# A residual load asked for eight halves later in one slot of an attention and expert block

## The chip, the cores and the metric

One core of one Trainium2 chip. The metric is the device time of one execution in microseconds, as the median of the runs shown. Lower is better.

## The reference, cut to what matters

The input x has 4 batches of 1024 tokens with 512 features. A block of attention (16 heads of 32) with a residual and a layer norm is followed by a routed low-rank expert block with a residual and a layer norm.

```python
xq, xk, xv = x @ wq.T, x @ wk.T, x @ wv.T             # split into 16 heads of 32
scores = einsum('bqhd,bkhd->bhqk', xq, xk)            # not scaled
probs = softmax(scores, axis=-1)
x = layernorm(x + einsum('bhqk,bkhd->bqhd', probs, xv).reshape(4, 1024, 512) @ wo.T)
# experts: E = 8, rank 64, out 512
logits = x @ Wr.T + br
h = einsum('nd,erd->ner', x, A)
y = einsum('ner,eor->neo', h, B) / 64
out = layernorm(x + y[argmax(logits)] * max(softmax(logits)))
```

## The kernel before

The attention of a pair of heads over one batch is a slot: 4 batches by 8 pairs are 32 slots, numbered 0 to 31. A slot has 16 units (8 blocks of keys by two heads), and a unit has two halves of 512 queries, so a slot has 32 halves, called h = 0 to 31 in the code. Each half makes one score product (`sc`, line 767), one exponential on ScalarE (`P`, line 894) and one product for the row maxima of the next slot (`mx`, line 757), which VectorE reduces (line 1034). Slot 8 is the first pair of the second batch, and slot 9 the second pair.

TensorE fills the room between the scores with chunks of other work by a plan that is written out at build time: projections of q, k and v (`w`, line 636), and in the slots of a later batch the output projection and the experts of the batch before. Slot 8 holds the projections of v of batch 1; slot 9 starts with the output projection of batch 0 (`o`, line 671), whose tiles VectorE adds to the residual in `r_f` (line 1134).

The denominators of the softmax go a longer way. GpSimd adds the 16 blocks of exponentials of a slot two by two into sums (lines 544 and 547), waiting for each unit's exponentials. In the next slot TensorE sums them over the keys (`den`, line 730), in slot 9 in the half h = 3; it waits there for the last add of slot 8. TensorE works through its program in order, so the attention product of slot 8 (`pv`, line 779) and the output projection stand behind it. VectorE copies the denominators (`den_s`, line 1075), SyncE spreads them over partitions (line 453), VectorE takes the reciprocals (line 1086), SyncE stores them to memory (`den_parts`, line 458) and, when the store has landed, loads them back to `den_s` (line 463). GpSimd multiplies the attention output with them in `normalise` (line 579), which waits for that load. For slot 7 this is at the half h = 19 of slot 8: `spread_den` is at h = 7, `store_rec` at h = 14, `load_rden` at h = 15. The adds of slot 8 that come later stand behind `normalise` on GpSimd.

SyncE also loads, in its one queue, the operands of the slots to come (`stack`, line 421): in slot 8 at h = 14, three transfers of 256 KB just ahead of `store_rec`. At h = 27 it issues four transfers of 4 KB with the maxima's rows (line 444); the first score of the next slot waits for them (`m_loaded`).

ScalarE issues the large loads in its own queue: the residual of the batch before, 2 MB (`load_res`, line 857), at h = 12 of slots 8, 16 and 24, and one more in slot 25; in slot 9 the experts' weights (line 865) at h = 1 and x for the next batch (line 845) at h = 3 and 9. `load_res(0)` waits for `qk_ready` 16 and for the stored slices of the weights, since `r` held the raw weights before. `load_res(1)` and `load_res(2)` wait for stored outputs. The only users of `r_loaded` are VectorE's additions in `add_attention` and `add_part`.

Of the kernel before, what the change touches and what calls it, by code (L numbers as in the profile page):

```python
# [6 lines left out]
def build_attention_lora_moe_block(nc, xT, x, wqT, wkT, wvT, woT, aT, bT, wrT, br, out):  # L7
# [130 lines left out]
    for s in range(SLOTS):  # L138
        chunks = [(kind, n, c) for kind, n in PLAN[s] for c in range(CHUNKS[kind])]
        begin, end, spent, total = FROM.get(s, 0), TO.get(s, HALVES), 0, sum(cost(kind) for kind, _, _ in chunks)  # L140
        for kind, n, c in chunks:
            half = HALVES * s + begin + int((end - begin) * (spent + cost(kind) / 2) / total)
            AT.setdefault(half, []).append((kind, n, c))
            if c + 1 == CHUNKS[kind]:
                ENDS.setdefault(half, []).append((kind, n))
            spent += cost(kind)
        ORDER += [piece for piece in PLAN[s] if piece[0] not in SHORT]
# [4 lines left out]
    for half in range(HALVES * SLOTS):  # L152
        s, h = divmod(half, HALVES)
# [46 lines left out]
    for half in range(HALVES * SLOTS):  # L200
        s, h = divmod(half, HALVES)
# [38 lines left out]
    def ends(half, kind):  # L240
        return [n for k, n in ENDS.get(half, ()) if k == kind]

    ctx = ExitStack()
    with ctx:
# [587 lines left out]
        def _(act):  # L832
# [6 lines left out]
            def load_x(b, c):  # L839
                if b and c == 0:  # L840
                    act.wait_ge(qk_ready, 16 * b)
                    act.wait_ge(v_ready, KB * b)
                elif c:
                    act.wait_ge(x_loaded[0], 16 * (b + 1))
                act.dma_start(xT_f[:, 1, :, 512 * c:512 * c + 512],
                             xT_w[:, :, S * b + 512 * c:S * b + 512 * c + 512]).then_inc(x_loaded[c], 16)

            def load_res(b):
                if b + 1 == B:
                    act.wait_ge(qk_ready, 16 * B)  # L850
                    act.wait_ge(v_ready, KB * B)
                elif b:
                    act.wait_ge(out_stored, 64 * b)
                else:
                    act.wait_ge(qk_ready, 16)
                    act.wait_ge(slices_stored, 32 * SLICES)
                act.dma_start(res(b), tokens(x, b, 0, KB)).then_inc(r_loaded, 16)

            def load_ab(b):

                act.wait_ge(v_ready, KB * (b + 1))
                if b == 1:
                    act.wait_ge(wv_stored, 16)
                for s, d in ((a_s, aT), (b_s, bT)):
                    act.dma_start(s, d.rearrange("(k p) n -> p k n", p=128)).then_inc(ab_loaded, 16)

            def load_wv(b):
                act.wait_ge(z_ready, KB * (b - 1))
                act.dma_start(wide[:, :, :, :].bitcast(f32), wv_d).then_inc(wv_loaded, 16)

            def x_high(b, m):
                c, kt = divmod(m, KT)
                act.wait_ge(x_loaded[c], 16 * (b + 1))
                act.activation(xT_s[:, 0, kt, 512 * c:512 * c + 512], xT_f[:, 1, kt, 512 * c:512 * c + 512],
                               ACT.Copy).then_inc(x_hi, 1)
# [9 lines left out]
            def exp(unit, c):  # L885
                if c == 0 and unit >= NP:
                    old, k = divmod(unit - NP, UNITS)
                    act.wait_ge(pv_done, (unit - NP) // 2 + 1)
                    if k < adds(old) + 2:
                        act.wait_ge(*summed(unit - NP))  # L890
                    else:
                        act.wait_ge(den_done, old + 1)
                act.wait_ge(sc_ready, 2 * unit + c + 1)
                act.activation(P[:, unit % NP, 512 * c:512 * c + 512], sc[c][:, :], ACT.Exp).then_inc(exp_done, 1)  # L894

            def hi_part(n):
                act.wait_ge(qk_ready, n + 1)
                before = n - (2 if n < 16 else 1)
                if before == 15:
                    act.wait_ge(qk_stored[0], 16 * 8)  # L900
                if before >= 0:
                    act.wait_ge(qk_stored[before % 2], 16 * (before // 2 + 1))
                act.activation(parts(n)[:, 0, :], BANK["qk", n][:, :], ACT.Copy).then_inc(hi_done, 1)

            def copy_v(n):
                act.wait_ge(v_ready, n + 1)
                if n >= KB:
                    act.wait_ge(pv_done, KB * (PAIRS * (n // KB) - 1) + n % KB + 1)
                act.activation(V[:, n % KB, :], BANK["v", n][:, :], ACT.Copy).then_inc(v_done, 1)

            def copy_out(s):
                act.wait_ge(pv_done, KB * (s + 1))
                if s > 1:
                    act.wait_ge(norm_done, 2 * (s - 1))
                act.activation(pv_s[:, s % 2, :], pv[:, :], ACT.Copy).then_inc(pv_copied, 1)  # L915

            def copy_max(q):
                act.wait_ge(mt_ready, q + 1)
                if q:
                    act.wait_ge(m_loaded, 64 * q)  # L920
                act.activation(mrow[:, 0, :], BANK["max_t", q][0:2 * KB, 0:128], ACT.Copy).then_inc(mhi_done, 1)

            def copy_yT(n, bank):
                act.wait_ge(t1_ready, n + 1)
                if n:
                    act.wait_ge(h_ready, n)
                act.activation(yT[:, :], bank[:, :], ACT.Copy).then_inc(yT_done, 1)

            def copy_hmT(n, bank):
                act.wait_ge(t2_ready, n + 1)  # L930
                if n:
                    act.wait_ge(z_ready, n)
                act.activation(hmT[:, :], bank[:, :], ACT.Copy, scale=SCALING).then_inc(hmT_done, 1)

            def softmax_sum(n):
                act.wait_ge(eq_done, n + 1)
                if n > 1:
                    act.wait_ge(lrec_done, n - 1)
                act.activation(lexp[:, :], logits[:, :], ACT.Exp, bias=nlmax[:, :], accum_out=lsum[:, n % 2:n % 2 + 1]).then_inc(lexp_done, 1)

            def layer_norm(kind, n):
                b, t = divmod(n, KB)
                act.wait_ge(nmr_done, NORM[kind, n] + 1)
                act.activation(res(b)[:, t, :], res(b)[:, t, :], ACT.Identity, bias=nmr[:, t:t + 1],
                               scale=rstd[:, t:t + 1]).then_inc(out_done if kind == "z" else y_done, 1)
# [27 lines left out]
            for half in range(HALVES * SLOTS):  # L973
                unit, c = divmod(half, 2)
                s, k = divmod(unit, UNITS)
                exp(unit, c)
                b, p, h = s // PAIRS, s % PAIRS, half % HALVES
                if half in LOAD_X:
                    load_x(*LOAD_X[half])
                if h == 12 and p == 0 and b:  # L980
                    load_res(b - 1)
                if h == 2 and p == 1 and b + 1 == B:
                    load_res(b)
                if h == 1 and p == 1 and b:
                    load_ab(b)
                if h == 2 and p == 7 and 0 < b < B - 1:
                    load_wv(b + 1)
                if half % HALVES == MAX_AT and s < LAST:
                    copy_max(s + 1)
                for n in ends(half - 4, "lg"):  # L990
                    softmax_sum(n)
                if c == 1 and k == 1 and s:
                    copy_out(s - 1)
                for kind, n in ENDS.get(half, ()):
                    if kind == "qk":
                        hi_part(n)
                    elif kind == "v":
                        copy_v(n)
                    elif kind == "t1":
                        copy_yT(n, BANK[kind, n])  # L1000
                    elif kind == "t2":
                        copy_hmT(n, BANK[kind, n])
                if half in X_HIGH:
                    x_high(*X_HIGH[half])
                for kind, late in (("o", 7), ("z", 11)):
                    for m in range(2):
                        for n in ends(half - late + m, kind):
                            if n % 2:
                                layer_norm(kind, n - m)
# [282 lines left out]
```

## Time and profile before

| | us |
|---|---|
| median of 3 runs | 1524.68 |
| lowest, highest | 1523.99, 1529.59 |
| the profiled execution | 1531.46 |
| its span | 1529.6 |

In the span TensorE is busy 1476.3 us (97%), GpSimd 1158.6 (76%), VectorE 935.0 (61%) and ScalarE 777.2 (51%); the mean granted clock of TensorE is 0.988 of full. The share of a busy engine is an average over the span, and single stops show only in the timeline. In the rows below the engines are PE (TensorE, PEld for its weight loads), DVE (VectorE), ACT (ScalarE), POOL (GpSimd) and SP (SyncE); SPq and ACTq are the issues of transfers on the queues of SyncE and ScalarE. L857 is line 857 of the kernel.

### The profile page before, as it was taken

How to read it: one execution, taken by the hardware profiler on the slowest of the kernel's cores; microseconds unless marked ns; L12 is line 12 of the kernel's file. 1: busy time of each engine (PE TensorE's matmuls, PEld its weight loads, DVE VectorE, ACT ScalarE, POOL GpSimd, SP SyncE). 2: the span in 40 equal slices, each digit the busy share in tenths (PEclk: the TensorE clock that was granted, in tenths of full speed). 3: DMA queues.
4: the chain of work that ended last, by engine and by line, in shares of the span. 5: the costliest groups of instructions: out<-in, count | busy, mean ns of one | idle time of the engine just before them, and what ended most of it. 6: DMA issues, size and time to landing. Idle time of an engine off the chain costs nothing.

```text
span 1529.6 us, 20559 instructions
## 1 busy us (share of the span) xinstructions
PE 1476.3 (97%) x6872; PEld 863.2 (56%) x6872; DVE 935.0 (61%) x1754; ACT 777.2 (51%) x1421; POOL 1158.6 (76%) x654
## 2 busy tenths in 40 slices
PE   7999999999899999999999999999999999999898
PEld 5755556656455655556655555555665555544354
DVE  6747666765466666666566565666556666564643
ACT  3455656655355554555556454554555555555332
POOL 0367879999698777877889887778888998889401
PEclk9999999999999999999999999999999999999999
DMA  7345634553522332326262233224335222111001
GB/s 225 106 129 152 218 80 142 152 155 89 172 60 59 91 102 65 112 77 215 57 181 67 83 85 105 84 69 137 121 103 159 49 49 57 52 40 36 8 14 42
DMA packets 80216, 153.13 MB, mean 100 GB/s; under 512 B 19040, under 2 KB 26224, under 8 KB 79728
## 3 DMA queue, kind: packets, MB, share of 16 engines
q1 hardware_dynamic: 67936, 125.07, 28.7%
q10 hardware_dynamic: 11840, 25.69, 5.1%
q8 instruction: 55, 0.90, 0.2%
q0 software_dynamic: 336, 1.07, 0.2%
q14 instruction: 49, 0.40, 0.1%
HBM read 102.52 MB, written 48.49 MB: 99 GB/s over the span
## 4 chain that ended last, share of the span: by engine, by line
PE 78%; issue 9%; POOL 7%; DVE 4%; ACT 1%; DMA 1%; SPq 0%; ACTq 0%; POOLq 0%; DVEq 0%
PE w L636 14%; PE pv L779 13%; PE sc L767 13%; PE mx L757 12%; PE w L671 6%; PE w L715 5%; PE w L702 5%; POOL Psum L547 4%; PE mx L730 2%; DVE mxc L1034 2%; POOL attT_f L579 1%; POOL Psum L544 1%; PE mx L715 1%; PE w L679 1%; PE mx L695 1%
## 5 line engine op out<-in xcount | busy, mean ns | idle before, releaser
L1034 DVE TENSOR_REDUCE mxc<-mx 128x1 f32<-128x512 f32 x1024 | 683.4, 686 | 472.6 <-PE mx L757 470.0
L894 ACT ACTIVATE P<-sc 128x512 f32<-128x512 f32 x1024 | 598.6, 596 | 516.7 <-PE sc L767 490.2
L547 POOL TENSOR_TENSOR Psum<-Psum,P 128x1024 f32<-128x1024 f32 x296 | 695.8, 2377 | 30.8 <-ACT P L894 28.5
L767 PE MATMUL sc<-stack 98*128 98x512 f32 x1024 | 539.2, 529 | 4.4 <-ACT P L894 4.0
L757 PE MATMUL mx<-stack 96*128 96x512 f32 x1024 | 405.0, 401 | 5.4 <-DVE mxc L1034 2.8
L767 PEld LDWEIGHTS sc<-stack 98*128 98x128 f32 x1024 | 194.2, 190 | 139.6 <-issue 83.2
L757 PEld LDWEIGHTS mx<-stack 96*128 96x128 f32 x1024 | 195.6, 191 | 115.6 <-issue 69.5
L779 PE MATMUL pv<-P,V 128*32 128x512 f32 x2048 | 252.7, 612 | 0.0
L636 PE MATMUL w<-xT_s,wqk_s 128*128 128x512 f32 x624 | 199.1, 410 | 12.0 <-DVE xT_s L1051 10.4
L544 POOL TENSOR_TENSOR Psum<-P 128x1024 f32<-128x1024 f32 x50 | 118.5, 2384 | 117.4 <-ACT P L894 108.9
L636 PEld LDWEIGHTS w<-xT_s,wqk_s 128*128 128x128 f32 x624 | 117.7, 193 | 70.0 <-issue 45.5
L779 PEld LDWEIGHTS pv<-P,V 128*32 128x32 f32 x2048 | 57.6, 111 | 131.5 <-issue 106.6
L636 PE MATMUL w<-wide,xT_s 128*128 128x512 f32 x384 | 114.0, 400 | 0.0
L702 PE MATMUL w<-wide_f,turned_f 128*128 128x512 f32 x208 | 108.0, 605 | 0.0
L547 POOL TENSOR_TENSOR xT_s_f<-xT_s_f,P 128x1024 f32<-128x1024 f32 x41 | 97.1, 2391 | 13.3 <-ACT P L894 12.9
L715 PE MATMUL w<-wide_f,turned_f 128*128 128x512 f32 x208 | 106.9, 599 | 0.1
L671 PE MATMUL w<-wo_s,attT_f 128*128 128x512 f32 x198 | 102.4, 599 | 0.0
L579 POOL TENSOR_TENSOR attT_f<-pv_s,den_s 64x512 f32<-64x512 f32 x62 | 80.1, 1291 | 25.5 <-issue 17.7
L636 PEld LDWEIGHTS w<-wide,xT_s 128*128 128x128 f32 x384 | 71.2, 190 | 28.4 <-issue 13.4
L547 POOL TENSOR_TENSOR wo_s<-wo_s,P 128x1024 f32<-128x1024 f32 x32 | 75.3, 2384 | 2.4 <-ACT P L894 2.1
L556 POOL TENSOR_TENSOR ve<-mv,eps_s 128x2 f32<-128x2 f32 (+1 forms) x33 | 6.5, 196 | 87.6 <-DVE mv L1123 87.6
L915 ACT ACTIVATE pv_s<-pv 128x512 f32<-128x512 f32 x32 | 19.1, 597 | 75.1 <-PE pv L779 75.1
(146 smaller groups left out, 1090.2 us busy)
## 6 DMA issues: line engine op xcount, KB each, us to landing
stack<-qk_parts SPq DMA_DIRECT2D x186, 256.0 KB, 4.3
qk_parts<-split SPq DMA_DIRECT2D x56, 512.0 KB, 3.3
wqk_s<-wqk_parts SPq DMA_DIRECT2D x24, 512.0 KB, 4.4
den_s<-den_parts SPq DMA_DIRECT2D x124, 64.0 KB, 2.0
xT_s_f<-xT ACTq DMA_DIRECT2D x6, 1024.0 KB, 6.8
r_f<-x ACTq DMA_DIRECT2D x3, 2048.0 KB, 12.8
out<-r_f SPq DMA_DIRECT2D x12, 512.0 KB, 3.4
qk_parts<-turned SPq DMA_DIRECT2D x8, 512.0 KB, 2.8
```

Source lines behind the costliest of these rows:

```text
L544: pool.tensor_tensor(sums(s)[:, i, :], P[:, (unit - 2) % NP, :], P[:, unit % NP, :], ALU.add).then_inc(add_done, 1)
L547: pool.tensor_tensor(sums(s)[:, i, :], sums(s)[:, i, :], P[:, unit % NP, :], ALU.add).then_inc(add_done, 1)
L579: pool.tensor_tensor(attT[64 * (p % 2):64 * (p % 2) + 64, p // 2, 512 * c:512 * c + 512], pv_s[64 * c:64 * c + 64, s % 2, :], den_s[64 * c ...
L636: return pe.matmul(bank[:, :], weights[i], moving[j], start=(c == 0), stop=(c == PASSES * KT - 1))
L671: done = pe.matmul(bank[:, :], attT[:, kt, 128 * t:128 * t + 128], wo_s[:, kt, :], start=(kt == 0 or only), stop=(kt == KT - 1))
L702: done = pe.matmul(bank[:, :], yT[:, 128 * kt:128 * kt + 128], a_s[:, kt, :], start=(kt == 0), stop=(kt == KT - 1))
L715: done = pe.matmul(bank[:, :], hmT[:, 128 * kt:128 * kt + 128], b_s[:, kt, :], start=(kt == 0), stop=(kt == KT - 1))
L757: pe.matmul(bank[:, :], stack(q, i)[0:3 * HD, 1, 128 * qb:128 * qb + 128], stack(q, i)[0:3 * HD, 0, 512 * c:512 * c + 512], start=True, st ...
L767: pe.matmul(sc[c][:, :], stack(s, i)[0:KS, 0, 128 * kb:128 * kb + 128], stack(s, i)[0:KS, 1, 512 * c:512 * c + 512], start=True, stop=True ...
L779: done = pe.matmul(pv[at:at + HD, :], V[:, kb, HD * head:HD * head + HD], P[:, (UNITS * s + 2 * kb + i) % NP, 512 * c:512 * c + 512], star ...
L894: act.activation(P[:, unit % NP, 512 * c:512 * c + 512], sc[c][:, :], ACT.Exp).then_inc(exp_done, 1)
L1034: dve.tensor_reduce(mxc[:, q % 2, at:at + 1], BANK["max", g][:, :], AX.X, ALU.max).then_inc(mx_done, 1)
```

## The change

`load_res(0)` is called in slot 8 at h = 20 instead of h = 12. The calls in slots 16 and 24 stay at h = 12, and the one in slot 25 stays where it is.

```diff
                 if half in LOAD_X:
                     load_x(*LOAD_X[half])
-                if h == 12 and p == 0 and b:
+                if h == (20 if b == 1 else 12) and p == 0 and b:
                     load_res(b - 1)
                 if h == 2 and p == 1 and b + 1 == B:
                     load_res(b)
```

## Rows read from the trace of the kernel before

**Rows 1.** The page, part 1: busy us (share of span) xinstructions of each engine.

```profile
PE 1476.3 (97%) x6872; PEld 863.2 (56%) x6872; DVE 935.0 (61%) x1754; ACT 777.2 (51%) x1421; POOL 1158.6 (76%) x654
```

**Rows 2.** Waits, 372 to 440 us: total us, times, longest us.

```profile
PE mx L730 <- POOL Psum L547: 6.8, 1, 6.8
```

**Rows 3.** Timeline of GpSimd: start us, us, instruction, count, [idle before <-releaser].

```profile
380.87 7.11 POOL L547 TENSOR_TENSOR Psum<-Psum,P 128x1024 f32<-128x1024 f32 x3 [0.57 <-ACT P L894]
395.88 2.64 POOL L579 TENSOR_TENSOR attT_f<-pv_s,den_s 64x512 f32<-64x512 f32 x2 [7.91 <-issue]
398.59 16.31 POOL L547 TENSOR_TENSOR Psum<-Psum,P 128x1024 f32<-128x1024 f32 x7
```

**Rows 4.** Timeline of TensorE's products at the start of slot 9.

```profile
407.81 0.39 PE L757 MATMUL mx<-stack 96*128 96x512 f32 x1
415.04 1.94 PE L730 MATMUL mx<-Psum,ones 128*32 128x512 f32 x8 [6.84 <-POOL Psum L547]
...
419.62 1.13 PE L671 MATMUL w<-wo_s,attT_f 128*128 128x512 f32 x2
```

**Rows 5.** Windows: length, busy us (x) of each engine, PEclk, DMA share, GB/s.

```profile
415.00:417.00 2.00, 1.96 (x12) 0.68 (x16) 0.00 (x0) 0.00 (x0) 0.00 (x0) 0.50 0.91 339
```

**Rows 6.** Timeline of SyncE's issues in slot 8.

```profile
380.19 1.65 SPq L421 DMA_DIRECT2D stack<-qk_parts  x3
381.88 0.52 SPq L458 DMA_DIRECT2D den_parts<-spread_s  x1
391.74 2.42 SPq L463 DMA_DIRECT2D den_s<-den_parts  x4
397.38 2.75 SPq L444 DMA_DIRECT2D stack<-mrow  x4
```

**Rows 7.** Transfers issued from 372 to 400: count, KB each, median us to landing.

```profile
r_f<-x ACTq DMA_DIRECT2D x1, 2048.0 KB, 12.8
stack<-qk_parts SPq DMA_DIRECT2D x3, 256.0 KB, 9.0
...
den_parts<-spread_s SPq DMA_DIRECT2D x1, 8.0 KB, 9.8
```

**Rows 8.** Timeline of ScalarE in slot 8: the residual's issue; the exponential of h = 20.

```profile
379.19 0.37 ACTq L857 DMA_DIRECT2D r_f<-x  x1
...
389.78 0.60 ACT L894 ACTIVATE P<-sc 128x512 f32<-128x512 f32 x1 [2.46 <-PE sc L767]
```

**Rows 9.** Timeline of SyncE's issues in slot 3 (first row) and slot 7.

```profile
155.59 0.42 SPq L458 DMA_DIRECT2D den_parts<-spread_s  x1
...
340.54 1.26 SPq L421 DMA_DIRECT2D stack<-qk_parts  x3
341.84 0.43 SPq L458 DMA_DIRECT2D den_parts<-spread_s  x1
346.56 1.71 SPq L463 DMA_DIRECT2D den_s<-den_parts  x4
```

**Rows 10.** Timeline of GpSimd: `normalise` in slot 3 and in slot 7.

```profile
163.43 2.65 POOL L579 TENSOR_TENSOR attT_f<-pv_s,den_s 64x512 f32<-64x512 f32 x2 [1.33 <-issue]
...
350.23 2.67 POOL L579 TENSOR_TENSOR attT_f<-pv_s,den_s 64x512 f32<-64x512 f32 x2 [1.26 <-issue]
```

**Rows 11.** Timeline of TensorE's weight loads: the first score of slot 9.

```profile
404.22 0.19 PEld L767 LDWEIGHTS sc<-stack 98*128 98x128 f32 x1
```

**Rows 12.** Timeline of TensorE at the same place in slot 17.

```profile
788.76 0.39 PE L757 MATMUL mx<-stack 96*128 96x512 f32 x1
789.08 1.07 PE L730 MATMUL mx<-Psum,ones 128*32 128x512 f32 x8
...
791.79 1.13 PE L671 MATMUL w<-wo_s,attT_f 128*128 128x512 f32 x2
```

**Rows 13.** Timeline of TensorE: `den` in slot 8.

```profile
369.62 1.07 PE L730 MATMUL mx<-Psum,ones 128*32 128x512 f32 x8 [0.48 <-POOL Psum L547]
```

**Rows 14.** Transfers of line 453 (`spread_s`) issued from 785 to 800, in slot 17.

```profile
DMA to landing us min/median/max: 5.3/5.4/5.7
```

## The prediction

> **What bounds the kernel now.** I read the page first: TensorE is busy for 1476.3 us of a span of 1529.6 [rows 1]. So the time is TensorE's own work, and a step that moves a load can only change a place where TensorE stands still or runs slowly. The list of waits for 372 to 440 us, the stretch of slot 8 and the start of slot 9, has one such place: TensorE's denominator product (`den`, line 730) waits 6.8 us for GpSimd's sums [rows 2]. GpSimd's timeline gives the reason. It ends a group of adds at 387.98 (380.87 + 7.11), starts `normalise` for slot 7 only at 395.88, after 7.91 us of "issue", and the seven adds that are left of slot 8 end at 398.59 + 16.31 = 414.90 [rows 3]. TensorE's last product before `den` ends at 408.20, and `den` starts at 415.04, 0.14 us after the last add [rows 4]. The view by windows shows what comes with the stop: from 415 to 417 the granted clock is 0.50 of full, 1.2 GHz instead of 2.4, after TensorE had stood still [rows 5]. `den` and the attention products behind it take from 415.04 to 419.62, that is 4.58 us [rows 4].
>
> What is `normalise` waiting for? "issue" says only that no engine of the profile released it. In the code it needs `add_done` (its own adds, done), `pv_copied` (a copy at the start of the slot) and `rden_loaded`, the reciprocals that SyncE loads back. SyncE's rows have the answer: the 8 KB store `den_parts` is issued at 381.88, and the load `den_s` behind it, which waits for that store, at 391.74 [rows 6]. The view of transfers gives 9.8 us from the store's issue to its landing and 9.0 for the `stack` transfers ahead of it on the same queue, beside a residual of 2 MB that took 12.8 [rows 7]; ScalarE had issued that at 379.19 [rows 8]. In slot 7, where the same four transfers follow each other with no residual, the load is issued 4.7 us behind the store (341.84 to 346.56) [rows 9].
>
> **The change part by part.** Nothing is added or removed. One transfer with its two waits moves from the 13th to the 21st half of slot 8, to behind the exponential at 389.78 [rows 8]. Its waits (`qk_ready` 16, `slices_stored`) were met slots before, so nothing new is queued behind them on ScalarE, and the issue (0.37 us) falls beside idle time there: the exponential at 389.78 came after 2.46 us of it. No step of SyncE or GpSimd is reordered.
>
> Step 1, the reciprocals come earlier. SyncE's stack issues at 380.19 are held by TensorE's score, which the change doesn't touch. The three issues took 1.65 us there and 1.26 in slot 7 [rows 6, 9]; without the residual I take slot 7's 1.30 from the first of them to the store, so it goes out at 381.5. From the store's issue to the start of `normalise` it is 8.39 us in slot 7 (341.84 to 350.23) and 7.84 in slot 3 (155.59 to 163.43) [rows 9, 10]. That gives 389.3 to 389.9; I take 389.6 instead of 395.88, a gain of 6.3 us. GpSimd is free by then (387.98). The upper bound of this unknown: the store still at 381.88, 4.7 to landing, and slot 8's own stretch from the load's issue to `normalise`, 4.14 (391.74 to 395.88): 390.7, a gain of 5.2.
>
> Step 2, GpSimd passes it on. From `normalise` to the end of the last add it is 414.90 - 395.88 = 19.02 us, back to back. The exponentials that the adds need don't hold them: the last one of slot 8 belongs to a score that TensorE made before slot 9's first, at 404.22 [rows 11], and its add would start at 408.6 - 2.3 = 406.3. So the sums end at 408.6, and `den` may start at 408.75.
>
> Step 3, what is late next. The same place in slot 17 shows TensorE with no such wait: from the start of the last maximum product to `den` 0.32 us, to the first output product behind it 3.03 (788.76 to 791.79) [rows 12]. Put on slot 9's 407.81 that is `den` at 408.13 and the output product at 410.84. It was at 419.62, so the whole stop is worth at most 8.78 us: 6.91 of waiting and 1.87 of slow clock (4.58 against 2.71 from `den` on). With `den` at 408.75 TensorE still waits 0.6 us for GpSimd. The gain is 415.04 - 408.75 = 6.29, and 1.87, together 8.16.
>
> Does the clock stay up? In slot 8 `den` followed a stop of 0.48 us and its eight products took 1.07 us [rows 13], as in slot 17; after 6.84 us they took 1.94 [rows 4]. A stop of 0.6 is nearest to the first, so I take the full 1.87 and keep zero as the other end.
>
> Step 4, what the residual now lies beside. It runs from 389.9 to about 402.7 (12.8 us again). The reciprocals' store and load are through by 390. Its user, VectorE's addition to the first output tile, comes behind `den` in slot 9, so after 411: at least 8 us to spare. What lies inside it are SyncE's four row transfers of the maxima, issued from 397.38 to 400.1 [rows 6]; slot 9's first score needs them, its weights are loaded at 404.22 [rows 11]. Their landing isn't shown. The nearest row is slot 17's: four small transfers of the same queue, issued while ScalarE's loads of 3 MB are under way, land 5.3 to 5.7 us after their issue [rows 14]. With 5.7 behind the last issue (about 399.5) that is 405.2: TensorE loses 1.0 us and reaches `den` at 409.1, a gain of 7.8 instead of 8.16, since most of it overlaps with the 0.6 that it would wait anyway. The other end is no loss. I take no loss, because the residual is through 1.5 us before the score.
>
> A rule that bears on this step: the Trainium skill, "DMA: Bandwidth & Descriptors", section "Queues, rings and completion order", says that each DMA engine takes turns between the queues, packet by packet. By it a small transfer alone in SyncE's queue waits for a few turns, not for the end of the residual; the sum would stay 8.16, and 7.8 would be too low. The trace agrees in so far as slot 17's small transfers landed while the loads were still under way (5.7 us), and the stack transfers took about twice their time, not the whole of the residual's (9.0).
>
> Behind slot 9 the engines beside TensorE wait for it, and slot 17 goes through the same order of work, with small transfers beside big loads, without a stop. So I let the whole gain reach the end. The profiled execution took 1531.46 us, of which 1529.6 is the span; it would take 1523.3. The runs shown have a median of 1524.68, 6.8 below the profiled one; the stop is a matter of the order of transfers and not of that difference, so the same 8.16 comes off: 1516.5.
>
> **The rivals.**
> A, a part of the gain stays away: the reciprocals come at 390.7 (upper bound of step 1), or the clock falls all the same. The gains are 5.2 + 1.87 = 7.1, or 6.29, or with both 5.2: 1517.6 to 1519.5. For it speaks that the way from the load to `normalise` is 4.14 us in slot 8 and 3.7 in slot 7 (346.56 to 350.23); against it, that slot 8's four load issues themselves took 2.42 instead of 1.71 [rows 6, 9].
> B, the edit doesn't do what it says: the store was late for another reason than the residual, the stack transfers ahead of it alone. `normalise` stays at 395.9 and the time at 1524.7. Against it speaks slot 7, in which the same three stand ahead [rows 9].
> C, slower: a wait for the maxima's rows takes the place of the one removed. Its place is slot 9's first score, 404.22. The price at worst: the four transfers are served one after the other, 5.7 us each from 397.38, until 420.2; TensorE stops for 16.0, the clock falls again (1.87), and the output product comes at 410.84 + 16.0 + 1.87 = 428.7 instead of 419.62, 9.1 later: 1533.8. It decides from the point where the last lands after 411.1 (404.22 + 8.78 - 1.87). Against it: in slot 17 the four landed side by side, and after 402.7 no load is left to hold them. The longest that a small one took in these rows is 9.8; that would give 409.3, a stop of 5.1, and with the slow clock still 1.8 us less than before.
>
> **How the numbers follow.** Forecast (a gain of 7.2 to 8.8): 0.72. A: 0.17. B: 0.07. C: 0.04. A measurement of this kernel can tell about 0.5% from no change, 7.6 us here. The forecast lies only 0.5 us beyond that line; the runs shown lie 5.6 us apart, so a median may be off by about 1, and I put two thirds of the forecast's cases beyond the line: faster 0.49, same 0.47 (the rest of the forecast, A, B), slower 0.04. The range: at the fast end the whole stop, 1524.68 - 8.78 = 1515.9, and 1.4 for the scatter, 1514.5; at the slow end A's 1519.5 and 1.5, 1521.0. B and C stay out.
>
> **What would show it.** Right: the residual is issued at about 389.9, the store `den_parts` lands 4 to 5 us after its issue, `normalise` starts at 389 to 390, `den` starts at 408.2 to 409.2 and takes 1.1 us, the granted clock has no dip behind it, and the first output product follows at 411 to 412. Step 1 is wrong if the store still takes over 7 us; step 4 if a wait stands before the first score of slot 9. The forecast as a whole is wrong if slot 9 starts its output products 8 us earlier and a later wait, on x or on the reciprocals of slot 8, has grown by as much.

## The result and the profile after

| | before | after |
|---|---|---|
| median, us (runs) | 1527.21 (7) | 1516.83 (7) |
| lowest, highest | 1523.99, 1532.98 | 1515.96, 1524.38 |
| profiled execution, its span | 1531.46, 1529.6 | 1524.38, 1522.6 |
| ratio to before | | 0.9941, 95% interval 0.9918 to 0.9963 |

The change takes 0.6% off, 9.0 us (5.7 to 12.5 by the interval). The forecast was 1516.5 and 8.2 us. Two of all the executions in this document, 2209.57 us and 3730.6, were slow runs and count in no ratio and no median.

In the changed kernel's timeline of SyncE the load follows the reciprocals' store by 4.66 us (383.22 to 387.88), as in slot 7, where it is 4.7; before it was 9.86. The columns are start, duration, instruction and count; the four rows answer to [rows 6].

```profile
381.93 1.25 SPq L421 DMA_DIRECT2D stack<-qk_parts  x3
383.22 0.43 SPq L458 DMA_DIRECT2D den_parts<-spread_s  x1
387.88 1.71 SPq L463 DMA_DIRECT2D den_s<-den_parts  x4
399.12 3.03 SPq L444 DMA_DIRECT2D stack<-mrow  x4
```

The view of transfers issued from 372 to 400, which answers to [rows 7]: the store lands after 4.6 us (9.8 before), the stack transfers after 4.7 (9.0), and the residual itself after 8.5 (12.8).

```profile
r_f<-x ACTq DMA_DIRECT2D x1, 2048.0 KB, 8.5
stack<-qk_parts SPq DMA_DIRECT2D x3, 256.0 KB, 4.7
...
den_parts<-spread_s SPq DMA_DIRECT2D x1, 8.0 KB, 4.6
```

The timelines of GpSimd (first two rows, [rows 3] of before) and of TensorE (the others, [rows 4]):

```profile
391.31 2.65 POOL L579 TENSOR_TENSOR attT_f<-pv_s,den_s 64x512 f32<-64x512 f32 x2 [1.60 <-issue]
394.04 16.47 POOL L547 TENSOR_TENSOR Psum<-Psum,P 128x1024 f32<-128x1024 f32 x7
```

```profile
409.55 0.39 PE L757 MATMUL mx<-stack 96*128 96x512 f32 x1
410.66 1.06 PE L730 MATMUL mx<-Psum,ones 128*32 128x512 f32 x8 [0.72 <-POOL Psum L547]
411.52 1.93 PE L779 MATMUL pv<-P,V 128*32 128x512 f32 x16
413.37 1.12 PE L671 MATMUL w<-wo_s,attT_f 128*128 128x512 f32 x2
```

`normalise` waits 1.60 us instead of 7.91, and the residual was issued only at 391.60, when `normalise` had started. TensorE waits 0.72 us instead of 6.84, its eight `den` products take 1.06 instead of 1.94, and from the last maximum product to the output product it is 3.82 us (409.55 to 413.37) where it was 11.81. That is 7.99 us. The view by windows shows the granted clock at full (PEclk, the third figure from the end, 1.00) where [rows 5] had 0.50:

```profile
408.00:412.00 4.00, 3.28 (x23) 1.50 (x25) 2.19 (x4) 1.75 (x3) 2.51 (x2) 1.00 0.99 260
412.00:416.00 4.00, 4.00 (x24) 1.79 (x17) 1.17 (x2) 1.20 (x2) 0.00 (x0) 1.00 1.05 386
```

The spans differ by 7.0, not by 7.99, because the changed kernel's profiled run happened to reach slot 8 about 2 us later: SyncE's first issue of slot 8 is at 361.51 against 359.50. A mark ahead of the stop that all kernels share is ScalarE's load of the experts' weights in slot 9. From it to the end of the span it is 1529.6 - 406.28 = 1123.3 us before and 1522.6 - 408.02 = 1114.6 after, so 8.7 us less.

### The profile page after: what moved, and what is told of

Its sections match the earlier page's. It is cut to its first block, busy times and chain, and to the rows that moved or that the text cites. A ratio compares the mean times of both kernels' runs of the same rounds, so it can differ in the third digit from the quotient of the medians.

```text
span 1522.6 us, 20559 instructions
## 1 busy us (share of the span) xinstructions
PE 1475.1 (97%) x6872; PEld 862.3 (57%) x6872; DVE 935.8 (61%) x1754; ACT 777.8 (51%) x1421; POOL 1158.7 (76%) x654
## 3 DMA queue, kind: packets, MB, share of 16 engines
q1 hardware_dynamic: 67936, 125.07, 29.1%
## 4 chain that ended last, share of the span: by engine, by line
PE 79%; issue 8%; POOL 6%; DVE 4%; DMA 2%; ACT 1%; SPq 0%; POOLq 0%; ACTq 0%; DVEq 0%
PE w L636 14%; PE pv L779 14%; PE sc L767 13%; PE mx L757 13%; PE w L671 6%; PE w L715 5%; PE w L702 5%; POOL Psum L547 4%; PE mx L730 2%; DVE mxc L1034 2%; POOL attT_f L579 1%; PE mx L715 1%; PE w L679 1%; PE mx L695 1%; DMA xT_s_f<-xT 1%
## 5 line engine op out<-in xcount | busy, mean ns | idle before, releaser
L636 PE MATMUL w<-xT_s,wqk_s 128*128 128x512 f32 x624 | 198.4, 409 | 11.7 <-DVE xT_s L1051 10.1
L579 POOL TENSOR_TENSOR attT_f<-pv_s,den_s 64x512 f32<-64x512 f32 x62 | 80.1, 1291 | 20.2 <-issue 12.5
## 6 DMA issues: line engine op xcount, KB each, us to landing
r_f<-x ACTq DMA_DIRECT2D x3, 2048.0 KB, 12.6
```

Source lines behind the costliest of these rows:

```text
L579: pool.tensor_tensor(attT[64 * (p % 2):64 * (p % 2) + 64, p // 2, 512 * c:512 * c + 512], pv_s[64 * c:64 * c + 64, s % 2, :], den_s[64 * c ...
L636: return pe.matmul(bank[:, :], weights[i], moving[j], start=(c == 0), stop=(c == PASSES * KT - 1))
```

## The experiments

The theory is that of the prediction: the residual and SyncE's transfers share the DMA engines, SyncE's queue is in order, and the late reciprocals reach TensorE over GpSimd's adds. The rivals were that the stack transfers alone hold the store (B), that small transfers under a big load are a new wait (C), that slot 8 is special, and that GpSimd itself sets the end. Each group of runs has its own runs of the kernel before beside it, so the medians of before differ a little from group to group. In kernels with added lines the line numbers are 2 to 5 higher.

**The residual at h = 16, between the two places.**

```diff
-                if h == 12 and p == 0 and b:
+                if h == (16 if b == 1 else 12) and p == 0 and b:
```

> The residual of the first batch is asked for at h = 16 of slot 8, 4 halves later than before and 4 earlier than in the change. Theory (transfers share the DMA engines, and SyncE's queue is in order): the store of the reciprocals, issued 2 us ahead of the residual, lands nearly as without it (5 to 6 us), but the four loads behind it are issued under the residual and land 5.4 us after their issue instead of 2.0, as slot 17's small transfers did. The normalisation of slot 7 starts 3 to 4 us later than in the changed kernel, the denominator product of slot 8 waits 4 us, its clock falls or not (that is open: between a stop of 2.4 us, behind which the eight products took 1.93, and 0.7). Time: 2.5 us less than before if the clock falls, 4.5 if not. Rival (the stack transfers ahead of the store are the cause, not the residual): as before, no gain.

Ratio 0.9980 (0.9963 to 0.9996), medians 1524.62 and 1528.08: 3 us less than before. The view of its transfers, and GpSimd's and TensorE's timelines:

```profile
den_s<-den_parts SPq DMA_DIRECT2D x4, 64.0 KB, 5.7
...
den_parts<-spread_s SPq DMA_DIRECT2D x1, 8.0 KB, 4.8
```

```profile
388.86 2.65 POOL L579 TENSOR_TENSOR attT_f<-pv_s,den_s 64x512 f32<-64x512 f32 x2 [5.91 <-issue]
```

```profile
408.09 1.94 PE L730 MATMUL mx<-Psum,ones 128*32 128x512 f32 x8 [4.90 <-POOL Psum L547]
409.77 2.59 PE L779 MATMUL pv<-P,V 128*32 128x512 f32 x16
412.29 1.13 PE L671 MATMUL w<-wo_s,attT_f 128*128 128x512 f32 x2
```

The store, issued at 376.47 and so 2.1 us ahead of the residual (378.60), takes 4.8 us, about as in the changed kernel, and the price passes on to the four loads behind it: 5.7 us in the median instead of 2.1. The stop is 4.90, and the clock falls behind it: from `den` to the output product 4.20 us against 2.71 in [rows 12]. So the stop changes with what lies under the residual, and B is refuted: the stack transfers stand ahead of the store in this kernel and in the changed one alike.

**The residual at h = 25, on top of the maxima's rows.** The same edit with 25.

> The residual is asked for at h = 25 of slot 8, two halves ahead of the four transfers of the maxima's rows on which slot 9's first score waits, so these lie inside it from start to end. Theory (small transfers of the other queue land side by side, 5.4 us after their issue): the last lands at 405 of before's time scale, the first score of slot 9 waits 0.5 to 1.5 us, and the gain is 7 to 8 us of the change's 8 to 9, since that wait overlaps with the one for GpSimd's sums. Rival C (they are served one after the other, or behind the residual): the first score waits 10 us or more and the time is 4 to 9 us above the changed kernel's, at worst above before's. The residual lands before its first user in both.

Ratio 0.9961 (0.9945 to 0.9977): 6 us less than before (3.5 to 8.4 by the interval), where I had said 7 to 8. TensorE's timeline at the first score of slot 9:

```profile
399.88 0.50 PE L767 MATMUL sc<-stack 98*128 98x512 f32 x1 [0.69 <-DMA stack<-mrow]
```

The four row transfers were issued from 391.95 on over 2.75 us, with the residual issued at 389.91; the last one landed at about 399.8, 5.8 us after its issue at about 394.0. The wait that the prediction's rival C named exists and costs 0.7 us. The four transfers aren't served one after the other at 5.7 us each. By these times alone they could still have waited for the end of the residual, which landed at 400.1. The DMA view by windows decides that: from 392 to 396 it has 640 packets of ScalarE's queue and none of SyncE's, and from 396 to 398 it has 60 of SyncE's small packets among 325 of ScalarE's. So the small transfers run beside the residual, but their first packet moves only 4.1 us after their issue. In the changed kernel the residual, issued at 391.60, had landed at 400.1, and the first score (its weights loaded at 405.96) waits for nothing.

**The residual at h = 12 as before, and slot 8's three stack transfers behind the reciprocals' loads.**

```diff
-                if h == (14 if s else 28) and s + 2 < SLOTS:
+                if s != PAIRS and h == (14 if s else 28) and s + 2 < SLOTS:
...
+                if s == PAIRS and h == 15:
+                    sp.wait_ge(sc_ready, half)
+                    load_stack(s + 2, 0)
```

> The residual stays at h = 12 of slot 8, as before, but the three stack transfers of 256 KB that stood ahead of the reciprocals' store in SyncE's queue (h = 14) are issued behind the reciprocals' loads, in slot 8 alone. Theory: the store is alone in its queue and shares the engines with the residual only, so it lands in 5.4 us instead of 9.8; the loads behind it are issued at about 386.7 and land in 2 to 5 us; the normalisation starts at 390 to 392 instead of 395.9. The stop of the denominator product shrinks from 6.8 to 1.5 to 3 us: 4 to 6 us less than before. If the store still takes 9 us or more, the residual alone holds a small transfer until its own end, and there is no gain.

Ratio 0.9948 (0.9927 to 0.9970), medians 1519.21 and 1528.08. The profile is that of the same kernel in the next group of runs:

> The residual at h = 12 as before, the three stack transfers of slot 8 behind the reciprocals' loads; now for a profile to read. The measured gain of this edit was nearly that of the change. Theory: the store, alone in its queue beside the residual, lands in 5.4 us, the four loads behind it in 2 to 5 us, the normalisation starts 4 to 5.5 us earlier than before counted from the residual's issue (16.7 us behind it before, 11 to 12.5 here), and the denominator product waits 1.5 to 3 us. If the store lands in 2 to 3 us, the residual alone doesn't hold a small transfer and the stack transfers ahead of it do it all.

Ratio 0.9943 (0.9916 to 0.9969). Its SyncE timeline, its transfers and TensorE's `den`:

```profile
379.36 0.35 SPq L458 DMA_DIRECT2D den_parts<-spread_s  x1
385.48 1.71 SPq L463 DMA_DIRECT2D den_s<-den_parts  x4
387.36 1.25 SPq L421 DMA_DIRECT2D stack<-qk_parts  x3
```

```profile
r_f<-x ACTq DMA_DIRECT2D x1, 2048.0 KB, 8.9
...
den_parts<-spread_s SPq DMA_DIRECT2D x1, 8.0 KB, 6.1
```

```profile
408.21 1.07 PE L733 MATMUL mx<-Psum,ones 128*32 128x512 f32 x8 [0.73 <-DVE mxc L1037]
```

(The row of `den` names VectorE, but GpSimd's last add ended at 408.07, 0.14 us ahead of it, as in the other kernels.) With the residual in its old place this edit gains about as much as the change. That is 8 to 9 us where I expected 4 to 6; the intervals reach down to 4.6 and 4.7. The store beside the residual alone takes 6.1 us, not 9.8. Since it goes out as soon as the reciprocal is made, and no longer behind three issues, the loads behind it are issued at 385.48, 8.2 us behind the residual's issue (377.25), where it was 12.6 before. Put together with the changed kernel (4.6 behind the stack transfers alone) and the next one (1.6 with neither), the 9.8 us were the work of both, the residual and the 768 KB ahead in the same queue.

The packets show where the 6.1 us go. The store is issued at 379.36, and the DMA view has no packet of SyncE's queue until 382.8, while 590 packets of ScalarE's queue move; then, from 382.8 to 385.2, it has the store's 144 packets among 381 of the residual's. With neither load nor stack transfers, in the next kernel, the same 144 packets begin 0.8 us after the issue and take 0.2 us. So most of the price is a wait of about 3.5 us before the first packet, and the rest are turns. In the kernel before it was the stack transfers, the first in SyncE's queue, that moved nothing from 380.2 to 384 (3.9 us), and then they and the store shared the engines with the residual until 391.3. What holds the first packets for so long is not shown.

**Both edits.** h = 20 and the stack transfers behind.

> Both: the residual at h = 20 and the three stack transfers behind the reciprocals' loads. The store lands in 2.2 us, as where nothing is ahead of it; the normalisation starts as soon as GpSimd's adds let it (the changed kernel waits 1.6 us more there), and the denominator product of slot 8 waits for nothing: 0.7 to 1.1 us less than the changed kernel, 8 to 9.5 less than before. If it is no faster than the changed kernel, the rest of its stop was not due to the queue.

Ratio 0.9948 (0.9927 to 0.9969), on three runs.

```profile
den_parts<-spread_s SPq DMA_DIRECT2D x1, 8.0 KB, 1.6
```

```profile
404.37 1.07 PE L733 MATMUL mx<-Psum,ones 128*32 128x512 f32 x8
```

The store lands in 1.6 us, `normalise` starts behind GpSimd's adds with no wait, and `den` starts 0.32 us behind the last maximum product, as in slot 17. The 0.7 us that TensorE still waits in the changed kernel are gone from the profile; they are too small for the measured times to show.

**The residual at h = 2, ten halves earlier.** The same edit with 2.

> The residual is asked for at h = 2 of slot 8, ten halves earlier than before, so that it is through before the reciprocals' store at h = 14. Theory (only the meeting of the residual with the store counts, not that it is late): the store lands in 4.6 us as in the change, the denominator product waits under 1 us, 8 us less than before. The spread of the denominators at h = 7 lies under the residual (5.4 us instead of 1.7), which nothing waits for until the reciprocal at h = 13. Rival (it gains only by being put off, for instance since it then meets fewer transfers in all): no gain, or less than half.

Ratio 0.9955 (0.9933 to 0.9977): 7 us less than before.

```profile
409.21 1.06 PE L730 MATMUL mx<-Psum,ones 128*32 128x512 f32 x8 [0.44 <-POOL Psum L547]
```

The store lands in 4.3 us, the residual in 8.2. One part of the expectation missed: the spread of the denominators was issued at 372.03, when the residual had landed (371.3), and took 1.7 us as before. Early is as good as late within the intervals; what counts is that the residual lies under neither the store nor the loads behind it. How close to them it may end was not measured.

The calls in slots 16 and 24 show the same without an edit. They stay at h = 12, but there `den` is at h = 3 and not at 6, so the store goes out at h = 11, ahead of the residual (757.92 and 761.05 in slot 16 of the kernel before), and the stack transfers at h = 14 come behind it. The store lands in 1.5 us. The residual and the stack transfers still slow each other there, 12.7 us and 8.8, and the list of waits from 760 to 800 has none for them.

**The residual in slot 7, at h = 12.**

```diff
-                if h == 12 and p == 0 and b:
-                    load_res(b - 1)
+                if (s == PAIRS - 1 and h == 12) or (h == 12 and p == 0 and b > 1):
+                    load_res(max(b - 1, 0))
```

> The residual is asked for at h = 12 of slot 7, a whole slot earlier, where it meets slot 7's store of the reciprocals just as it met slot 8's. Theory: slot 8 and 9 run as in the change, but the same stop appears one slot earlier: slot 7's store lands in 9 to 10 us, its normalisation starts 5 to 6 us later than in the kernel before, and the denominator product of slot 7 (in slot 8, h = 6) waits 5 to 6 us, with the slow clock behind it. Time: within 2 us of before. Rival (slot 8 is special): as fast as the change.

Ratio 0.9979 (0.9963 to 0.9994): 3 us less than before (0.9 to 5.7 by the interval), where I had said within 2. The transfers issued from 338 to 355, GpSimd, and the waits from 340 to 385 (total, times, longest):

```profile
den_parts<-spread_s SPq DMA_DIRECT2D x1, 8.0 KB, 10.4
```

```profile
356.16 2.59 POOL L579 TENSOR_TENSOR attT_f<-pv_s,den_s 64x512 f32<-64x512 f32 x2 [7.18 <-issue]
```

```profile
ACT split L903 <- DMA qk_parts<-split: 6.0, 1, 6.0
...
PE sc L767 <- ACT P L894: 4.8, 1, 4.8
```

The store is as late as in slot 8 (10.4), and so is GpSimd (7.18). But TensorE's stop is not at `den` (377.52, no wait), where I had put 5 to 6 us. In slot 7 SyncE has stores of `qk_parts` to issue behind the reciprocals' loads; while it waits for the late store they wait too, ScalarE waits 6.0 us for the buffer that they empty, and TensorE's score stands behind ScalarE for 4.8 us. The granted clock is 0.50 behind this stop too (358 to 360). The theory holds for the cause and nearly for the size, and missed the road: I had followed the late transfer along one consumer only, not along the queue.

**The residual at h = 12 as before, `den` of slot 8 two halves later.**

```diff
         def den_at(s):
+            if s == PAIRS + 1:
+                return 5
```

> The residual stays at h = 12 as before; the denominator product of slot 8 and all that hangs on it is put two halves later in slot 9 (h = 5 instead of 3), so that TensorE has the last attention product of slot 8 (1.9 us) and two halves of other work (2.6 us) to do while GpSimd is late. Theory (the cost is TensorE's stop at this one product): GpSimd's sums end as late as before, the stop shrinks from 6.8 to 2 to 2.5 us, and 4.5 us are gained, 5 to 6 if the clock falls for a shorter time. Rival (GpSimd itself is what the end waits for): no gain, the lost time comes back in later waits of slot 9.

Ratio 0.9940 (0.9920 to 0.9960). In the profile `normalise` is as late as before (a wait of 7.56 us) and the store as slow (10.0), but TensorE's stop is short:

```profile
410.87 1.80 PE L732 MATMUL mx<-Psum,ones 128*32 128x512 f32 x8 [1.88 <-POOL Psum L549]
```

From the weights' load in slot 9 to the end of the span it is 1518.8 - 402.37 = 1116.4, so 6.9 us less than before in this profile, nearer to my 4.5 to 6 than the 9 us of the medians. So GpSimd's delay by itself costs little or nothing. The cost is that TensorE comes to the product that needs GpSimd before GpSimd is ready, and has nothing else to do.

**A version beyond the change.** The profiles of before and after have a second stop of this kind, `den` of slot 6 in slot 7 (2.13 us before, 2.42 after). Two kernels move that `den` two halves later, one of them with the stack transfers put back as well, beside the change once more.

```diff
         def den_at(s):
+            if s == PAIRS - 1:
+                return 8
```

> The change itself once more, as the measure for the two kernels beside it: 0.994 of before, 8 to 9 us less.

> The change, and in slot 7 the denominator product of slot 6 with all that hangs on it two halves later (h = 8 instead of 6). In the profiles of before and of the change TensorE waits there 2.1 to 2.4 us for GpSimd's sums, once with and once without a slow clock behind it. Theory (TensorE has two halves, 2.3 us, of other work to do in that time): the stop shrinks to under 0.5 us, GpSimd is no later than now, and the kernel takes 2 to 3.5 us less than the change, 10 to 12 less than before. Rival (GpSimd is full in slots 5 to 7, so the lost time comes back at the next denominator product, in slot 8): no faster than the change.

> The kernel beside it, with slot 8's three stack transfers behind the reciprocals' loads as well. Theory: the rest of the wait for the denominator product of slot 8 (0.7 us) goes too: 0.5 to 1 us less than the kernel beside it, within the measurement's scatter.

| | median | ratio to before (1530.94) | interval |
|---|---|---|---|
| the change again | 1521.16 | 0.9928 | 0.9902 to 0.9954 |
| and `den` of slot 6 later | 1518.05 | 0.9911 | 0.9890 to 0.9933 |
| and slot 8's stack transfers behind | 1517.08 | 0.9915 | 0.9895 to 0.9936 |

The two `den` products in slots 7 and 8, of the second kernel:

```profile
327.99 1.06 PE L732 MATMUL mx<-Psum,ones 128*32 128x512 f32 x8 [0.71 <-POOL Psum L549]
...
365.16 1.06 PE L732 MATMUL mx<-Psum,ones 128*32 128x512 f32 x8 [1.40 <-POOL Psum L549]
```

and of the change in the same group of runs:

```profile
330.45 1.94 PE L730 MATMUL mx<-Psum,ones 128*32 128x512 f32 x8 [2.15 <-POOL Psum L547]
...
370.76 1.07 PE L730 MATMUL mx<-Psum,ones 128*32 128x512 f32 x8 [0.64 <-POOL Psum L547]
```

The stop in slot 7 shrinks by 1.44 us, to 0.71 and not to under 0.5, and its slow clock is gone, and 0.76 us come back in slot 8: both the theory and its rival are in part right. Both versions are faster than before beyond doubt; against the change their 3 to 4 us lie within the intervals.

## Why the prediction was right

The mechanism came as forecast at every step, and the sizes of steps 1 to 3 too; the signs that the prediction set are all met once the profile's times are moved by the 1.7 us that it runs late (389.6 for `normalise`, 408.9 for `den`, 411.6 for the output product). That the median is within 0.4 us of the 1516.5 is luck. The forecast took 8.16 off a median of 1524.68 of three runs; the seven runs of before have 1527.21, so the base was 2.5 too low, and the medians differ by 10.4.

Step 1, the reciprocals: right in both parts. From SyncE's first stack issue to `normalise` I had 389.6 - 380.19 = 9.4 us; it is 391.31 - 381.93 = 9.4, and 15.7 before. One row that I read for it carries the wrong name: the store at 155.59 and the `normalise` at 163.43 are of slot 2, not of slot 3. Nothing hung on the number of the slot.

Step 2, GpSimd: 19.02 us from `normalise` to the last add were expected and 394.04 + 16.47 - 391.31 = 19.20 measured.

Step 3, what is late next: a wait of 0.6 was expected and 0.72 measured, the clock stayed up, and the output product came 3.82 us behind the last maximum product, where my figures say 3.65. The estimate of the whole, 8.16, stands against 7.99 at this place and 8.7 to the end of the span. The other 0.7 is not explained, and it is less than two profiles of the changed kernel differ by (1114.6 and 1112.1 from the same mark); of the kernel before there is one profile.

Step 4, what the residual lies beside: right in its outcome, no wait before slot 9's first score. One term was mis-sized. I took the residual's 12.8 us from before, as if they were its own; they held the share of the stack transfers. With nothing large beside it it takes 8.5 (8.4 with both edits), though 9.9 in the changed kernel's second profile. So it was through at 400.1, 5.9 us ahead of the score's weight load and not 1.5; in the second profile it was 4.5. It changed no sum, but it is why the maxima's rows were never near. The 5.7 us that I took for a small transfer under a load was nearly the right bound: h = 25 shows 5.8, h = 16 up to 6.1, and the store alone in its queue took 6.1. The turns between the queues, by which the prediction put such a transfer at a few turns, are there in the packets; most of its time is the wait ahead of the first of them.

Rival A did not come, though its clock part is real in this kernel: see below. B fell with h = 16, and in its strong form with the change itself. Yet it held a part of the truth that my text left aside: the stack transfers ahead of the store were a condition of the 9.8 us, and removing them does as well as moving the residual. C has its place and a price of 0.7 us, far from the point from which it decides.

The chances were about even between faster by over 0.5% and within it, and the measured 0.59% lies just beyond the line, which its interval (0.37% to 0.82%) crosses. So the side of the line is luck too.

The scatter behind that can be read in part. In kernels that are alike up to there, SyncE's first issue of slot 8 lies between 354.4 (h = 25) and 361.5 us (the change). Of these 7.1 us, 4.0 are there by the first `den` (98.6 and 102.6), and 2.9 come between `den` in slot 7 and slot 8, where the clock fell in the one and stayed up in the other. Over whole executions the time goes with the mean granted clock: the kernel before took 1522.96 us at 0.995 and 1535.60 at 0.986, the change 1513.53 at 0.997 and 1526.19 at 0.989. At an equal 0.992 they took 1525.44 to 1528.79 (eight runs of before) and 1520.33 and 1521.16 (the change), about 7 us apart.

## What to carry to other kernels

As these runs show it for reciprocals, a small transfer that a chain of work waits for costs little alone, but a multiple when a big load of another queue and some loads ahead of it in its own queue share the engines with it: look at its time to landing at each of its places, and put the big load before or behind it. Then look at who stands behind it in order, on the issuing queue as well as among its readers, since the stop shows at the engine that comes, in its own order, to something that isn't ready. Either end of the chain can be moved: the big load, the loads ahead, or the product that waits.

## What the runs showed of the hardware

A load of 2 MB took 8.2 to 9.9 us with nothing large beside it, 10.1 beside four loads of 64 KB (h = 16) or at h = 25, and 12.7 to 13.1 beside 768 KB of another queue. That queue's 256 KB transfers took 8.8 to 9.4 us (medians) in the same time and 4.1 to 4.7 without the load. Transfers of 4 to 64 KB under such a load took 5.3 to 6.1 us instead of 1.6 to 2.1, and slot 17's of 2 KB, under loads of 3 MB, 5.3 to 5.7 instead of 1.7. SyncE's first packet came 3.5 to 4.3 us after its issue at the seven places looked at where a big load of ScalarE's queue was under way, and 0.8 to 1.1 us after it at the eight without. In every kernel in which the store lay under the residual, the store landed 0.3 to 0.6 us ahead of it; by these times alone it might have been held to the residual's end, but its packets run between the residual's.

The clock behind a short stop isn't settled by the stop's length alone. The `den` of slot 6 waited 2.13 us in the kernel before, and its products took 1.93; in the kernel with h = 16 the same product waited 2.16 us and took 1.06. Rows of TensorE in slot 7, before and h = 16:

```profile
330.41 1.93 PE L730 MATMUL mx<-Psum,ones 128*32 128x512 f32 x8 [2.13 <-POOL Psum L547]
```

```profile
327.10 1.06 PE L730 MATMUL mx<-Psum,ones 128*32 128x512 f32 x8 [2.16 <-POOL Psum L547]
```

After 1.88 us it had fallen in the kernel with `den` two halves later, whose products in slot 7 took 1.06 after a stop of 2.49; after 0.72 and 0.73 it stayed up; after 4.90 and 6.84 it fell. From `den` in slot 7 to SyncE's first issue of slot 8 it is 27.7 and 28.2 us in the three profiles in which the clock stayed up there, and 29.1 to 31.4 in the five in which it fell. So by these rows a stop of around 2 us costs itself, and 1 to 4 us more when the clock falls behind it, an estimate; which of them comes varies from run to run.
